# Two products of the first attention written in pairs with 64 columns of weights

## The chip, the cores and the metric

The kernel runs on one core of a Trainium2 chip. The metric is the device time of one execution in microseconds (us), as the median of several runs. A core has TensorE (in the profile PE for the matmuls and PEld for the loads of weights), VectorE (DVE), ScalarE (ACT), GpSimd (POOL) and SyncE (SP), each with a queue of instructions of its own, and 16 DMA engines. The engines meet through semaphores.

## The reference

Four attention blocks run one after the other over x of shape (64, 64, 128): 64 sequences of 64 tokens with 128 features. The change lies in the first of them, a cross attention with relative positions. Its core, cut to what matters:

```python
kv = jnp.concatenate([memory, layer_input], axis=1)          # 128 tokens: 64 of the memory, 64 of x
q = (layer_input @ Wq).reshape(b, q_len, n_head, d_head)     # 16 heads of 64
k = (kv @ Wk).reshape(b, kl, n_head, d_head)
v = (kv @ Wv).reshape(b, kl, n_head, d_head)
r = (pe @ Wr).reshape(kl, n_head, d_head)
ac = jnp.einsum('bqhd,bkhd->bhqk', q + content_bias, k)
bd = rel_shift(jnp.einsum('bqhd,khd->bhqk', q + position_bias, r))
attn = jax.nn.softmax((ac + bd) * (1.0 / np.sqrt(d_head)), axis=-1)
ctx = jnp.einsum('bhqk,bkhd->bqhd', attn, v).reshape(b, q_len, n_head * d_head)
out = layer_norm(layer_input + ctx @ Wo, ln1_g, ln1_b)
```

Its feed-forward part, a second block with two attentions, a third with a gate and a fourth with two attentions and a mixture of experts follow. They are not touched.

## The kernel before

The first attention walks over 32 tiles. A tile is two sequences, so 2 x 64 queries lie on the 128 partitions. The kernel doesn't compute v and the output projection one after the other. It multiplies Wv and Wo of each head once, at the start, into a table VO of 16 matrices of 128x128 (L598). For each tile it then needs, for head h and sequence b, the product of the tokens and the probabilities (128 features x 64 queries), and then the sum over the heads of that product times VO[h]. These two are the products that are changed:

- L536: for each half G of the heads (8 heads) and each sequence b, one f32 matmul with the tokens kv_in (128 tokens x 128 features) as weights and the probabilities of 8 heads x 64 queries, 512 columns, as the moving side. Four a tile; they write four banks of PSUM, j + 1 modulo 4. ScalarE copies each bank into pkvT (L749) and signals.
- L555: for each of the 16 heads one f32 matmul with pkvT[:, h] (128 features x 128 queries) as weights and VO[:, h] as the moving side, 128 columns. All sixteen add up in one bank. VectorE adds the sum to x (L690).

In the profile each f32 matmul has two records of a load and two of a matmul.

The order of TensorE's work is written out by hand in l0_tensor. A helper, walk_ahead, calls one function for each tile n; has(d) is true where tile n + d exists, so work for four tiles is in flight in one call. In a call TensorE does in this order: L499, 16 transposes of the probabilities of tile n; L515, the scores of tile n + 1, 32 products with 64 rows and 64 columns of weights, in all four quarters of the array; L528, two transposes of the tokens of tile n + 3; L536 for tile n; L548, 8 products with w_q for tile n + 3; L555 for tile n; L572, 16 products with 64 rows, for the relative positions of tile n + 3; L1199 (a helper for products in parts), the keys of tile n + 3, 24 records of 256 columns. The transposes at L528 and the products at L536 and L548 wait for semaphores of VectorE and ScalarE between them: probsT_kept (VectorE has copied the transposed probabilities, L663), kv_kept (VectorE has rounded the tokens into two parts, L675 and L679) and pkvT_kept. The first three calls and the last ones leave out what has no tile: tiles 0 to 28 have all parts, tiles 29 to 31 lack L528, L548, L572 and L1199, and tile 31 lacks L515 too. In the second attention L959 is a product that has 128 rows and 64 columns of weights already, after the transposes at L952.

The stage ends in a meeting of all engines (the function meet), and the next stage begins behind it.

Of the kernel before, what the change touches and what calls it, by code (L numbers as in the profile page):

```python
# [35 lines left out]
S = 64  # L36
D = 128
H = 16
# [110 lines left out]
def build(nc, a, out):  # L149
# [7 lines left out]
    with ctx:  # L157
        def sb(name, shape, dt=F32):
            return ctx.enter_context(nc.sbuf_tensor("sb_" + name, shape, dt))
# [3 lines left out]
        def sem(name):  # L163
            if name not in sems:
                sems[name] = ctx.enter_context(nc.semaphore("is_" + name))
            return sems[name]

        PS = ctx.enter_context(nc.psum_tensor("PS", [P, 8, 512], F32))
# [38 lines left out]
        with ExitStack() as first:  # L207
            VO, rel_bias, w_q0, w_k0_hi, w_k0_lo, rT, probs, probsT, pkvT = (
                first.enter_context(nc.sbuf_tensor("sb_" + name, shape, dt))
                for name, shape, dt in (("VO", [P, H, P], F32), ("rel_bias", [P, H, KL + 1], F32),  # L210
                                        ("w_q0", [P, H * DK], F32), ("w_k0_hi", [P, H * DK], F32R),
                                        ("w_k0_lo", [P, H * DK], F32R), ("rT", [P, H // 2, KL], F32),
                                        ("probs", [P, H, KL], F32), ("probsT", [P, H, P], F32),
                                        ("pkvT", [P, H, P], F32)))
# [119 lines left out]
        kv_in = sb("kv_in", [P, 4, 2, D])  # L334
# [120 lines left out]
        def l0_tensor(e, c):  # L455
# [9 lines left out]
            for q in range(2):  # L465
                o = bank()
                for i in range(4):
                    ch = 4 * q + i
                    ins = e.matmul(o[:, i * KL:(i + 1) * KL], wr[:, 2 * ch:2 * ch + 2], peT, start=True, stop=True)
                ins.then_inc(sem("l0_table_done"), 1)  # L470
            e.wait_ge(sem("l0_gap_wide"), 1)
            for g in range(4):
                o = bank()
                r = slice(DK * (g % 2), DK * (g % 2) + DK)
                if g == 0:
                    e.wait_ge(sem("l0_table_drained"), 2)
                for i in range(4):
                    ch = 4 * (g // 2) + i
                    ins = e.matmul(o[:, i * P:(i + 1) * P], gap_wide[r, ch], rT[r, ch], start=True, stop=True)
# [4 lines left out]
            def step(k, u, has):  # L484
# [3 lines left out]
                if has(0):  # L488
                    for g in range(4):
# [8 lines left out]
                        for i in range(4):  # L498
                            ins = e.transpose(PS[:, g, i * P:i * P + P], probs[:, 4 * g + i], ident[:, :])  # L499
                        ins.then_inc(sem("l0_probsT_done"), 1)  # L500
                if has(1):
# [3 lines left out]
                    for ch in range(H // 2):  # L505
                        i = ch % 4
                        for hh in range(2):
                            g, r = 2 * (ch // 4) + hh, slice(DK * hh, DK * hh + DK)
# [5 lines left out]
                            for b in range(2):  # L514
                                ins = e.matmul(PS[S * b:S * b + S, 4 + g, i * KL:i * KL + KL],  # L515
                                               q0T[r, v1, ch, S * b:S * b + S], k0T[r, v1, ch, KL * b:KL * b + KL],
                                               start=True, stop=True, skip_group_check=True)
                            if i == 3:
                                ins.then_inc(sem("l0_scores_done"), 1)
                if has(3):  # L520
# [6 lines left out]
                    for b in range(2):  # L527
                        ins = e.transpose(PS[:, 0, b * KL:b * KL + KL], kv_in[:, (u + 3) % 4, b], ident[:, :])  # L528
                    ins.then_inc(sem("l0_kvT_done"), 1)
                if has(0):  # L530
                    for j in range(4):
                        G, b = j // 2, j % 2
                        e.wait_ge(sem("l0_probsT_kept"), 2 * n + (1 if j == 0 else 2))
                        if j == 3 and has(3):
                            e.wait_ge(sem("l0_kv_kept"), 2 * (n + 3) + 2)
                        e.matmul(PS[:, (j + 1) % 4], kv_in[:, u, b], probsT[:, 8 * G:8 * G + 8, S * b:S * b + S],  # L536
                                 start=True, stop=True).then_inc(sem("l0_pkv_done"), 1)
                if has(3):
                    t = n + 3
                    e.wait_ge(sem("l0_kv_kept"), 2 * t + 1)  # L540
                    for half in range(2):
# [4 lines left out]
                        for i in range(4):  # L546
                            ch = 4 * half + i
                            ins = e.matmul(PS[:, 1 + half, i * P:i * P + P], w_q0[:, P * ch:P * ch + P], x_own,  # L548
                                           start=True, stop=True)
                        ins.then_inc(sem("l0_q_done"), 1)  # L550
                if has(0):
                    for j in range(H):
                        if j % 8 == 0:
                            e.wait_ge(sem("l0_pkvT_kept"), 4 * n + (3 if j == 0 else 4))
                        ins = e.matmul(PS[:, 3, 0:D], pkvT[:, j], VO[:, j], start=(j == 0), stop=(j == H - 1))  # L555
                    ins.then_inc(sem("l0_out_done"), 1)
                if has(3):
                    t = n + 3
                    for half in range(2):
                        e.wait_ge(sem("l0_q_kept"), 2 * t + half + 1)  # L560
                        for i in range(4):
                            ch = 4 * half + i
                            for hh in range(2):
                                g, r = 2 * half + hh, slice(DK * hh, DK * hh + DK)
                                if i == 0:
# [4 lines left out]
                                    elif has(2):  # L570
                                        e.wait_ge(sem("l0_rel_kept"), 4 * (n + 2) + g + 1)
                                ins = e.matmul(PS[:, 4 + g, i * KL:i * KL + KL], q0T[r, v3, ch], rT[r, ch],  # L572
                                               start=True, stop=True, skip_group_check=True)
# [3 lines left out]
                    for j in range(4):  # L577
# [8 lines left out]
                        for i in range(2):  # L586
                            at = P * (2 * j + i)
                            ins = product_in_parts(e, PS[:, j, 2 * KL * i:2 * KL * i + 2 * KL],
                                                   (w_k0_hi[:, at:at + P], w_k0_lo[:, at:at + P]),
                                                   (x_hi0[:, :], x_lo0[:, :]))  # L590
                        ins.then_inc(sem("l0_k_done"), 1)
                if isinstance(n, int) and n == -3:
                    e.wait_ge(sem("l0_vo_loaded"), 32)
                    for g in range(4):
                        e.wait_ge(sem("l0_rel_kept"), g + 1)
                        for i in range(4):
                            h = head_at(4 * g + i)
                            ins = e.matmul(PS[:, 4 + g, i * P:(i + 1) * P], wvT[:, h], wo0[:, h], start=True, stop=True)  # L598
                        ins.then_inc(sem("l0_table_done"), 1)
            walk_ahead(e, NT, step)  # L600
            e.wait_ge(sem("bases"), 1)
            for i, n in enumerate(("sa", "ca")):
                ins = e.matmul(PS[:, 2, P * i:P * i + P], bv_wide[:, i], w_out[n][:, :], start=True, stop=True)
# [592 lines left out]
        def product_in_parts(e, o, left, right):  # L1196

            for i, (l, r) in enumerate(((0, 0), (0, 1), (1, 0))):
                ins = e.matmul(o, left[l], right[r], start=(i == 0), stop=(i == 2))  # L1199
            return ins  # L1200
# [796 lines left out]
```

## Time and profile before

| | |
|---|---|
| median of 3 runs | 1948.61 us (1948.49 to 1951.13) |
| profiled execution | 1958.74 us |
| its span, first to last instruction | 1957.2 us |
| PE busy | 1623.2 us, 83% |
| PEld busy | 1297.1 us, 66% |
| DVE busy | 1360.1 us, 69% |
| ACT busy | 1171.2 us, 60% |
| POOL busy | 944.9 us, 48% |
| mean granted clock of TensorE | 0.904 |

The first attention takes about the first 620 us of the span. The profile gives the start of each instruction and its length; those of matmuls are pipelined, so the lengths of neighbours overlap, and the cost of one in a row is the distance of the starts. A row of the view in order of time merges neighbours of one kind: its first number is the start of the first, its second the time to the end of the last, and x is how many there are. Brackets at its end, if any, are idle time of the engine ahead of it.

### The profile page before, as it was taken

Reading aid. Unit: us, or ns where it says so; the run is one execution under the profiler, and the core shown is the slowest. Engines: PE = TensorE matmul, PEld = TensorE weight load, DVE = VectorE, ACT = ScalarE, POOL = GpSimd, SP = SyncE. Lnnn points to the kernel's source line nnn. Section 1 sums busy time; section 2 is a strip of 40 time slices with the busy share of each in tenths; the row PEclk is TensorE's granted clock in tenths of the full one; section 3 lists DMA queues with packets and bytes.
Section 4 is the critical chain, followed back from the end, with each engine's and each line's share of the span. In section 5 each row is a group of like instructions: output and inputs, shape, how many; then the busy total and the mean of one; then the engine's idle time right before and its main releaser. Section 6 shows DMA issues by size and latency. Waiting matters only on the chain. (4 is left out here: it accounts for less than half of the span.)

```text
span 1957.2 us, 54686 instructions
## 1 busy us (share of the span) xinstructions
PE 1623.2 (83%) x17114; PEld 1297.1 (66%) x17114; DVE 1360.1 (69%) x4172; ACT 1171.2 (60%) x3299; POOL 944.9 (48%) x1373
## 2 busy tenths in 40 slices
PE   6899999999996969999998764379998895439992
PEld 6788888888884747767776641157776674437771
DVE  3777777777775648888776538868887774337873
ACT  2776777677764437778776322258887771127771
POOL 2354344444532445556664424434454444646773
PEclk8999999999998979999998877779999995559996
DMA  8866666766661022230000000000000000136665
GB/s 228 159 149 144 155 148 139 160 142 153 146 148 45 0 103 106 100 110 21 19 18 8 1 1 1 0 4 1 0 10 13 12 9 21 43 99 206 220 211 163
DMA packets 214820, 167.19 MB, mean 85 GB/s; under 512 B 27633, under 2 KB 188785, under 8 KB 214449
## 3 DMA queue, kind: packets, MB, share of 16 engines
q1 hardware_dynamic: 206128, 142.88, 29.3%
q0 software_dynamic: 8576, 22.88, 3.6%
q8 instruction: 59, 0.97, 0.2%
q14 instruction: 57, 0.46, 0.1%
HBM read 91.92 MB, written 73.76 MB: 85 GB/s over the span
## 5 line engine op out<-in xcount | busy, mean ns | idle before, releaser
L738 ACT ACTIVATE sb_probs<-sb_probs,sb_work 128x128 f32<-128x128 f32 x512 | 198.6, 405 | 117.4 <-DVE sb_work L641 117.4
L281 POOL TENSOR_SCALAR sb_next_var_eps<-sb_next_moments 128x1 f32<-128x1 f32 (+1 forms) x184 | 45.3, 246 | 422.3 <-DVE sb_next_moments L721 241.9
L890 POOL TENSOR_TENSOR sb_work<-sb_work,sb_cols 128x512 f32<-128x512 f32 x128 | 134.1, 1048 | 216.2 <-ACT sb_work L1107 134.2
L1033 DVE TENSOR_REDUCE sb_work<-PS 128x8 f32<-128x512 f32 x256 | 175.2, 684 | 46.6 <-PE PS L932 44.9
L1035 DVE TENSOR_TENSOR sb_work<-PS,sb_work 128x512 f32<-128x512 f32 x256 | 177.0, 691 | 8.8
L1067 ACT ACTIVATE sb_work<-sb_work 128x512 f32<-128x512 f32 x256 | 161.5, 631 | 32.8 <-DVE sb_work L1035 26.8
L906 PE MATMUL PS<-sb_ident,sb_work 128*128 128x128 f32 x1024 | 151.0, 288 | 15.4 <-ACT sb_work L1107 9.9
L959 PEld LDWEIGHTS PS<-sb_v_ones,sb_work 128*64 128x64 f32 x4096 | 133.0, 140 | 24.0 <-issue 15.8
L959 PE MATMUL PS<-sb_v_ones,sb_work 128*64 128x18 f32 x4096 | 144.9, 214 | 4.3 <-ACT sb_work L1073 2.8
L1073 ACT ACTIVATE sb_work<-PS 128x512 f32<-128x512 f32 x256 | 139.6, 595 | 10.3 <-PE PS L906 7.0
L906 PEld LDWEIGHTS PS<-sb_ident,sb_work 128*128 128x128 f32 x1024 | 115.0, 146 | 42.7 <-issue 30.5
L433 POOL TENSOR_TENSOR sb_work<-sb_rel_bias,sb_work 128x2064 f32<-128x2064 f32 x32 | 134.7, 4210 | 5.2 <-POOL sb_work L431 4.2
L285 POOL TENSOR_TENSOR sb_tile_inv_std<-sb_next_var_eps,sb_half_power 128x1 f32 (+3 forms) x184 | 118.6, 644 | 7.2 <-POOL sb_next_var_eps L281 0.2
L555 PE MATMUL PS<-sb_VO,sb_pkvT 128*128 128x128 f32 x1024 | 119.9, 275 | 0.0
L1849 POOL DMA_INDIRECT expert_outs<-sb_work x92 | 96.5, 1049 | 47.3 <-issue 37.6
L555 PEld LDWEIGHTS PS<-sb_VO,sb_pkvT 128*128 128x128 f32 x1024 | 116.9, 192 | 2.3 <-ACT sb_pkvT L749 2.3
L536 PE MATMUL PS<-sb_probsT,sb_kv_in 128*128 128x512 f32 x256 | 117.3, 602 | 0.4 <-DVE sb_probsT L663 0.4
L641 DVE CUSTOM_DVE_ANT_0 sb_probs<-PS,sb_work 128x128 f32<-128x128 f32 x512 | 112.4, 285 | 4.2 <-DMA sb_work<-rel_scratch 4.2
L738 ACT ACTIVATION_READ_ACCUMULATOR sb_probs<-sb_probs,sb_work 128x1 f32 x512 | 104.4, 204 | 0.0
L771 ACT ACTIVATE sb_work<-PS 128x512 f32<-128x512 f32 x128 | 76.2, 598 | 44.7 <-PE PS L1199 34.0
L656 DVE TENSOR_TENSOR sb_work<-PS,sb_work 128x512 f32<-128x512 f32 x128 | 79.6, 683 | 32.8 <-PE PS L572 26.5
L1825 DVE CAST sb_h_hi<-sb_work 128x512 fp32r<-128x512 f32 x92 | 57.8, 628 | 53.9 <-ACT sb_work L1801 50.5
(276 smaller groups left out, 4454.4 us busy)
## 6 DMA issues: line engine op xcount, KB each, us to landing
rel_scratch<-sb_work SPq DMA_DIRECT2D x64, 516.0 KB, 7.8
sb_work<-rel_scratch SPq DMA_DIRECT2D x64, 512.0 KB, 6.6
expert_rows<-sb_blank SPq DMA_DIRECT2D x36, 520.0 KB, 2.9
sb_w_up<-expert_halves SPq DMA_DIRECT2D x23, 512.0 KB
sb_w_down<-expert_halves SPq DMA_DIRECT2D x23, 512.0 KB
expert_halves<-sb_e_halves POOLq DMA_DIRECT2D x16, 512.0 KB, 6.1
sb_work<-expert_rows SPq DMA_DIRECT2D x23, 260.0 KB
sb_e_raw<-e_W POOLq DMA_DIRECT2D x16, 256.0 KB, 5.5
```

The source lines that it names most:

```text
L285: e.tensor_tensor(inv_std[:, bass.ds(t0, tiles)], var_eps[:, 0:tiles], half_power[:, 0:tiles], ALU.pow)\
L433: e.tensor_tensor(masked_bias, rel_bias[:, :, :], mask_f.unsqueeze(1).to_broadcast([P, H, KL + 1]), ALU.add)\
L536: e.matmul(PS[:, (j + 1) % 4], kv_in[:, u, b], probsT[:, 8 * G:8 * G + 8, S * b:S * b + S], start=True, stop=True).then_inc(sem("l0_pkv_do ...
L555: ins = e.matmul(PS[:, 3, 0:D], pkvT[:, j], VO[:, j], start=(j == 0), stop=(j == H - 1))
L738: ins = e.activation(probs[:, j], probs[:, j], ACT.Exp, bias=neg_max[:, j:j + 1], scale=-1.0, accum_out=row_sum[:, j:j + 1])
L890: e.tensor_tensor(k_masked[:, u3], k_sb[:, u3].rearrange("p (b k) -> p b k", b=2).unsqueeze(2) .to_broadcast([P, 2, 4, S]), col("place").u ...
L906: ins = e.transpose(PS[:, 4 + j, i * P:i * P + P], att_probs[:, u, 8 * j + 2 * i:8 * j + 2 * i + 2], ident[:, :])
L959: ins = e.matmul(values[S * b:S * b + S, 2 * i:2 * i + 2], att_probsT[:, i, S * b:S * b + S], v_ones[:, u, b, 2 * i:2 * i + 2], start=True ...
L1033: e.tensor_reduce(top, mine, AX.X, ALU.max).then_inc(sem("att_max_ready"), 1)
L1035: e.tensor_tensor(by_group(att_probs[:, v])[:, 2 * j:2 * j + 2], mine, top.unsqueeze(3).to_broadcast([P, 2, 4, S]), ALU.subtract)\
L1067: e.activation(att_probs[:, v, 8 * j:8 * j + 8], att_probs[:, v, 8 * j:8 * j + 8], ACT.Exp, scale=front["scale"]).then_inc(sem("att_exp_do ...
L1073: e.activation(att_probsT[:, 4 * j:4 * j + 4].rearrange("p i q -> p (i q)"), PS[:, 4 + j], ACT.Copy)\
```

## The change

At L536 each product is cut in two along the features: the first takes the tokens' features 0 to 63 as weights and writes partitions 0 to 63 of the bank, the second takes features 64 to 127 and writes partitions 64 to 127. The moving side is the same 512 columns for both. The signal is given by the second. At L555 each product is cut in two along the queries, which are one sequence each: 64 columns of pkvT as weights, 64 partitions of the sum as output, with the same VO[:, j] as moving side. What is computed is the same, and no wait is added or taken away.

```diff
-                        e.matmul(PS[:, (j + 1) % 4], kv_in[:, u, b], probsT[:, 8 * G:8 * G + 8, S * b:S * b + S],
-                                 start=True, stop=True).then_inc(sem("l0_pkv_done"), 1)
+                        for half in range(2):
+                            r = slice(D // 2 * half, D // 2 * half + D // 2)
+                            ins = e.matmul(PS[r, (j + 1) % 4], kv_in[:, u, b, r], probsT[:, 8 * G:8 * G + 8, S * b:S * b + S],
+                                           start=True, stop=True, skip_group_check=True)
+                        ins.then_inc(sem("l0_pkv_done"), 1)
...
-                        ins = e.matmul(PS[:, 3, 0:D], pkvT[:, j], VO[:, j], start=(j == 0), stop=(j == H - 1))
+                        for b in range(2):
+                            ins = e.matmul(PS[S * b:S * b + S, 3, 0:D], pkvT[:, j, S * b:S * b + S], VO[:, j],
+                                           start=(j == 0), stop=(j == H - 1), skip_group_check=True)
```

## Rows read from the trace of the kernel before

**Rows 1.** The page: the span in 40 slices, busy tenths and granted clock of PE.
```profile
PE   6899999999996969999998764379998895439992
...
PEclk8999999999998979999998877779999995559996
```

**Rows 2.** Busy time of each engine in one stretch, with granted clock and DMA.
```profile
core 0: us, PE busy (x) PEld busy (x) DVE busy (x) ACT busy (x) POOL busy (x), PEclk, DMA share, GB/s
100.00:500.00 400.00, 400.00 (x4357) 342.22 (x4356) 301.56 (x1204) 283.88 (x1071) 188.42 (x210) 1.00 0.67 149
```

**Rows 3.** Waits of PEld, 200 to 500 us: total, times, longest (PE has none).
```profile
PEld PS L536 <- issue: 18.5, 80, 0.2
...
PEld PS L536 <- DVE sb_x_lo L679: 6.5, 17, 0.6
```

**Rows 4.** PE in order of time, L555 of one tile to L555 of the next.
```profile
304.14 3.74 PE L555 MATMUL PS<-sb_VO,sb_pkvT 128*128 128x128 f32 x32
307.81 2.06 PE L572 MATMUL PS<-sb_rT,sb_work 64*128 64x128 f32 x32
309.80 0.39 PE L1199 MATMUL PS<-sb_x_hi,sb_w_k_hi 128*128 128x256 f32 x1
...
312.75 1.91 PE L499 MATMUL PS<-sb_ident,sb_probs 128*128 128x128 f32 x16
314.59 1.98 PE L515 MATMUL PS<-sb_work 64*64 64x128 f32 x64
316.50 0.44 PE L528 MATMUL PS<-sb_ident,sb_kv_in 128*128 128x128 f32 x2
316.77 3.60 PE L536 MATMUL PS<-sb_probsT,sb_kv_in 128*128 128x512 f32 x8
320.20 1.95 PE L548 MATMUL PS<-sb_work,sb_w_q 128*128 128x128 f32 x16
321.99 1.28 PE L555 MATMUL PS<-sb_VO,sb_pkvT 128*128 128x128 f32 x10
```

**Rows 5.** By line, 200 to 500 us: duration ns min/median/max.
```profile
L515 PE MATMUL PS<-sb_work x1088: 269/269/321, 207.4 to 494.8; 64*64 64x128 f32 x182
...
L572 PE MATMUL PS<-sb_rT,sb_work x544: 272/272/373, 200.6 to 488.1; 64*128 64x128 f32 x182
...
L536 PE MATMUL PS<-sb_probsT,sb_kv_in x136: 592/592/659, 209.6 to 498.3; 128*128 128x512 f32 x136
...
L555 PE MATMUL PS<-sb_VO,sb_pkvT x518: 275/275/275, 199.8 to 486.1; 128*128 128x128 f32 x173
...
L528 PE MATMUL PS<-sb_ident,sb_kv_in x34: 272/300/329, 209.3 to 495.2; 128*128 128x128 f32 x34
...
L1199 PE MATMUL PS<-sb_x_hi,sb_w_k_hi x136: 279/282/390, 202.6 to 490.9; 128*128 128x256 f32 x136
```

**Rows 6.** Records in 0.05 us: L515, L959; columns as in rows 2, PE and PEld.
```profile
314.57:314.62 0.05, 0.03 (x4) 0.04 (x4) 1.00 0.77 175
...
1001.13:1001.18 0.05, 0.04 (x2) 0.04 (x2) 1.00 0.00 0
```

**Rows 7.** PE in order of time, L952 and L959; then L959 by line there.
```profile
1000.94 0.27 PE L952 MATMUL PS<-sb_ident,sb_work 128*128 128x128 f32 x1
1001.14 1.11 PE L959 MATMUL PS<-sb_v_ones,sb_work 128*64 128x18 f32 x32
...
L959 PE MATMUL PS<-sb_v_ones,sb_work x32: 211/211/232, 1001.1 to 1002.0; 128*64 128x18 f32 x32
```

**Rows 8.** L536 in order of time in the last two tiles, 30 and 31.
```profile
597.82 3.70 PE L536 MATMUL PS<-sb_probsT,sb_kv_in 128*128 128x512 f32 x8
...
609.92 5.40 PE L536 MATMUL PS<-sb_probsT,sb_kv_in 128*128 128x512 f32 x8 [0.44 <-DVE sb_probsT L663]
```

**Rows 9.** The loads (PEld) of L536's fourth product, in order of time.
```profile
318.97 0.19 PEld L536 LDWEIGHTS PS<-sb_probsT,sb_kv_in 128*128 128x128 f32 x1 [0.29 <-DVE sb_x_lo L679]
319.35 0.19 PEld L536 LDWEIGHTS PS<-sb_probsT,sb_kv_in 128*128 128x128 f32 x1 [0.19 <-issue]
```

## The prediction

> **What bounds the kernel now.** I read the slices of the page first. The first attention lies in the first third of the span, and there TensorE (PE) is at nine tenths or more in nearly every slice, at full clock (the 9s of PEclk) [rows 1]. Then one stretch of 400 us in the middle of this stage: PE 400.00 of 400.00 us, granted clock 1.00, VectorE 301.56, ScalarE 283.88, GpSimd 188.42, DMA 0.67 [rows 2]. A busy PE is not yet a bound PE, because the ends of matmuls are modelled, so I looked for waits. In 200 to 500 us the view has none of PE itself. PEld (the loads) stands idle 18.5 us for "issue" on L536 and 6.5 us for VectorE's L679, in 17 pieces [rows 3]. These are loads that stand ready behind a long stream (L536 streams 0.43 us, its load takes 0.19), so they cost PE nothing. The third proof is the pace itself. In order of time one tile goes L499, L515, L528, L536, L548, L555, L572, L1199, and L555 starts at 304.14 and again at 321.99, that is 17.85 us per tile, and no row has an idle piece in brackets [rows 4]. So each 0.1 us that PE gains or loses in a tile of this loop moves the end of the stage by 0.1 us, as often as the loop is full. The stage ends in a meeting of all engines, so nothing later takes it back.
>
> **What a record costs.** An f32 product is two PE records. Pace = (busy of the group minus the length of one record) / (records minus 1). L555: (3.74 - 0.275)/31 = 0.112 us per record. L548: (1.95 - 0.275)/15 = 0.112. L499: (1.91 - 0.273)/15 = 0.109. L536, 512 columns: (3.60 - 0.592)/7 = 0.430 [rows 4, 5]. 0.430/512 is 0.84 ns per column, so 128 columns need 0.107 us for the stream alone, whatever the weights are. L515 works in tiles of 64x64, L572 in tiles of 64x128 and L959 (second stage) in 128x64, the form that the change uses. Members of a group start together: in 0.05 us there are four records of L515 and two of L959 [rows 6]. L515's 64 records are 16 groups of four: (1.98 - 0.27 - 0.02 - 0.05)/15 = 0.109 us per group, where 0.02 is the stagger in a group and 0.05 is explained below. L572's 16 pairs: (2.06 - 0.27 - 0.01 - 0.10)/15 = 0.112 [rows 4, 5]. So tiles do run side by side, but a group costs what one full-array record costs.
>
> **What a change of tile shape costs.** This is the heart of it. Where no shape changes, the next group starts in step: L536 to L548 (320.20 - 316.77)/8 = 0.429, L548 to L555 (321.99 - 320.20)/16 = 0.112 [rows 4]. Where it changes there are two losses. First, the gap: L499 to L515 takes 314.59 - 312.75 = 1.84 for 16 records that need 16 x 0.109 = 1.75, so 0.09 more; L555 to L572 takes 3.67 for 32 x 0.112 = 3.58, again 0.09; L952 to L959 takes 0.20 where 0.11 is the pace, again 0.09 [rows 4, 7]. Second, the load of the first record is not hidden. The first record is longer than the others by what its load has to do: L515 321 against 269 (0.05, 64 columns of weights), L572 373 against 272 (0.10, 128 columns), L1199 390 against 282 (0.11, 128 columns), L528 329 against 272 (0.06, a transpose) [rows 5], L959 232 against 211 (0.02, 64 columns) [rows 7]. The end of the loop has it for L536 itself: behind L515 its eight records take 3.70 instead of 3.60 [rows 4, 8].
>
> The Trainium skill states this in "TensorEngine Tiling (Array Packing)", Tiling Modes: changing the mode, not only the tile, drains the engine. By that rule the change cannot be free here, and the trace agrees, with its 0.09 us; if shapes changed for nothing, the sum would be the small gain of (5) below alone, -0.08 us per tile and 1946 us. [...]
>
> **The change part by part.**
> (1) L536, probabilities times tokens: four products (eight records of 512 columns) become eight (sixteen records in eight pairs). A pair streams the same 512 columns, so 0.43 us per pair, as before, plus one stagger of 0.01. The loads get shorter, 64 columns, but they were hidden behind 0.43 us of stream. Gain 0.
> (2) Entering it from L528, which stays a full-array transpose: new change of shape, 0.09 + 0.05 (64 columns, as L515). Between 0.11 (with L959's 0.02) and 0.20 (with L572's 0.10). I take 0.14: the stream behind the load is long, as in L515.
> (3) Leaving it for L548, full array and 128 columns of weights: new, 0.09 + 0.10 = 0.19. Between 0.15 (L528's 0.06) and 0.20 (L1199). I take 0.19, L536 behind L515 being the same kind of load.
> (4) Entering L555 from L548: new, 0.14, bounds as in (2), plus a stagger of 0.01.
> (5) L555, 16 products (32 records of 128 columns) become 32 in 16 pairs (32 pair records). Its pace was 0.112; the stream's floor is 0.107, and L515, which has 64-column loads and 128-column streams, goes at 0.109. Gain 32 x 0.003 = 0.08. Bounds: 0 (pace as L572) and 0.16 (pace 0.107). I take L515's, the same sizes.
> (6) L555 to L572: a change of shape already, now from another shape. 0.
> (7) PE's other instructions: 8 + 32 more matmuls with their loads in a tile. L515 issues four loads and four matmuls per 0.109 us [rows 4], the pairs need half of that. 0. Waits and signals stay; each signal hangs on the last product of its pair, which ends 0.01 us later.
> Sum per tile: 0.14 + 0.01 + 0.19 + 0.14 + 0.01 - 0.08 = 0.41 us, so 17.85 becomes 18.26. The low end is 0.11 + 0.15 + 0.11 - 0.16 = 0.21. The high end is 0.20 + 0.20 + 0.20 = 0.60, with no gain in (5).
>
> Full tiles are those that have L548 behind L536, tiles 0 to 28 of 32: 29 x 0.41 = 11.9 us. Tiles 29 and 30 have L515 directly ahead of L536 and L555 directly behind [rows 8], so the shape changes there anyway, with a shorter load (0.05 less), then none, then L555 0.08 less, then a new change to L499 (0.09 + 0.06): about 0. The last tile adds one entry and one exit, of which part lies in waits that PE has there (0.44 us ahead of L536 [rows 8]): 0.3. Sum 12.2 us.
>
> **What is late next.** Nothing. VectorE, ScalarE and GpSimd are idle for 25, 29 and 53% of the stage [rows 2]. The one signal that is near is VectorE's L679, which releases the fourth product of L536: its load comes at 318.97, at 0.29 us after the engine was free, needs 0.11, and the stream behind it begins at 319.35 [rows 9], 0.27 us later than it could. In some tiles this is just too late: the longest record of L536 took 659 ns against 592 [rows 5]. The change delays that stream by 0.15 us and leaves L679's own start where it was, so this can only get better (0.2 us in all, not counted). The granted clock is at its level of 2.4 GHz in this stage and PE gets more to do, not less [rows 2].
>
> **Against the medians.** The profiled execution had a span of 1957.2 us and 1958.74 in all, the runs without the profiler a median of 1948.61, which is 0.5% less. The sum is one of instruction times in a stage at constant clock, so I add it to both: 1958.74 gives 1970.9, 1948.61 gives 1960.8.
>
> **Rivals.**
> (A) Faster. If L555's 0.112 were set by the load of 128 columns and not by the stream, loads of 64 columns in parallel would bring the pace of a pair toward L959's, which is (1.11 - 0.21 - 0.03)/15 = 0.058 [rows 7]. That is 32 x 0.054 = 1.73 us gained per tile against 0.49 of changes of shape, -1.2 us x 29 = -36 us: 1913 us. It wins from a pace under 0.112 - 0.49/32 = 0.097. Against it: L515 has the short loads and still needs 0.109, and L536 shows 0.107 for 128 columns. L959 streams only 18 columns. 5%.
> (B) Streams of two 128x64 tiles don't run side by side when they are long (all 128 rows are read twice, from the same addresses). L959's pairs start together but their 18 columns prove little. Then a pair of L536 takes 0.86 and one of L555 0.22: 8 x 0.43 + 32 x 0.107 = 6.9 us x 32 = 220 us, 2180 us. Against it: L515's groups of four include two column tiles on each half of the rows, each with its own stream, at full pace. 3%.
> (C) The loads of a pair are not hidden, since both members lie on the same rows: 0.05 us on each of 40 pair records, 2 us a tile, 64 us on top of the forecast's 12, 2025 us. Against it: L555 and L499 hide their loads on the same rows today, and L959's pace of 0.058 is less than a load of 0.05 and a stream of 18 x 0.84 ns = 0.015 together. 3%. The Trainium skill says in "TensorE: Matmul & The Clock Gate", Part 3, that loads overlap running matmuls only where the row group differs, which would give this case; the trace speaks against it, with L555's 0.112.
> (D) No difference. The loss of 0.09 may belong to changes of rows and not of columns, or the program may keep the full array's shape, or the cost hides in time that PE has. Against it: L952 to L959 changes columns alone and shows the gap, and PE shows no wait. Under 0.13 us per tile (3.9/29) it would be within what can be told, so about 1949. 5%.
>
> **How the numbers follow.** Forecast 84%: 1960.8. Its terms' ends, 0.21 and 0.60 per tile, times 29 and with 0 to 0.3 at the end give 6.1 to 17.7 us, 1954.7 to 1966.3. The three runs differ by 2.6 us among themselves, but not all terms will stand at one end, so I take 1955 to 1967. That holds nearly all of the forecast's own 84% and nothing of the rivals, about 8 in 10. A measurement of this kernel can tell 0.2%, 3.9 us, from no change. Slower 84 + 3 + 3 = 90%, same 5%, faster 5%.
>
> **What the changed profile would show.** L536 and L555 as 128*64 forms with twice the records, two starting together; L536's eight pairs still 0.43 apart and L555's at 0.109; the first record of L536 and L555 0.05 longer, L548's first 0.10 longer; gaps of 0.09 more at three places; 18.26 us from L555 to L555; all later stages shifted and otherwise equal. The forecast is wrong if L555's pace is far from 0.109 (A or C), if L536's pairs are not 0.43 apart (B), or if the first records are no longer than the rest (D).

## The result and the profile after

The changed kernel takes 1983.33 us (median of 4 runs, 1980.89 to 1985.28) where the kernel before takes 1949.87 on the same chip: a ratio of 1.0161, interval 1.0137 to 1.0185. It is slower, as forecast, but by 33.5 us and not by 11 to 12, and 1983.33 lies far outside 1955 to 1967.

First what went as forecast. PE in order of time for one full tile after the change (start us, length us, line; L538 is what L536 was, L551 what L548 was, L559 what L555 was, L577 and L1204 what L572 and L1199 were), to be held against [rows 4]:

```profile
300.98 3.71 PE L559 MATMUL PS<-sb_VO,sb_pkvT 128*64 128x128 f32 x64
304.62 2.06 PE L577 MATMUL PS<-sb_rT,sb_work 64*128 64x128 f32 x32
...
309.56 1.91 PE L499 MATMUL PS<-sb_ident,sb_probs 128*128 128x128 f32 x16
...
313.31 0.44 PE L528 MATMUL PS<-sb_ident,sb_kv_in 128*128 128x128 f32 x2
313.68 3.66 PE L538 MATMUL PS<-sb_probsT,sb_kv_in 128*64 128x512 f32 x16
317.26 2.05 PE L551 MATMUL PS<-sb_work,sb_w_q 128*128 128x128 f32 x16
319.25 2.29 PE L559 MATMUL PS<-sb_VO,sb_pkvT 128*64 128x128 f32 x38
```

From L559 to L559 it is 319.25 - 300.98 = 18.27 us, against a forecast of 18.26. By piece, the distance of starts after minus before: L528 to L538 0.37 - 0.27 = +0.10, L538 to L551 3.58 - 3.43 = +0.15, L551 to L559 1.99 - 1.79 = +0.20, L559 to L577 3.64 - 3.67 = -0.03. Sum +0.42. A load that isn't hidden lengthens the first record of its group, so it shows in the distance to the next group. Sorted that way the forecast's terms are 0.09, then 0.05 + 0.01 + 0.09 = 0.15, then 0.10 + 0.09 = 0.19, then 0.05 + 0.01 - 0.08 = -0.02: each is right to 0.01. The same by line, duration in ns min/median/max, from 300 to 358 us, to be held against [rows 5]:

```profile
L538 PE MATMUL PS<-sb_probsT,sb_kv_in x48: 592/592/644, 313.7 to 353.3; 128*64 128x512 f32 x48
...
L551 PE MATMUL PS<-sb_work,sb_w_q x58: 275/275/378, 299.8 to 355.6; 128*128 128x128 f32 x58
...
L559 PE MATMUL PS<-sb_VO,sb_pkvT x232: 272/273/323, 301.0 to 357.9; 128*64 128x128 f32 x116
```

The first record of L538 is 0.05 longer than the rest, that of L551 0.10, that of L559 0.05. L538's pairs are still (3.66 - 0.59 - 0.06)/7 = 0.430 apart, L559's (3.71 - 0.27 - 0.06)/31 = 0.109.

Now what did not. The slices of PE on the page after show nothing of it: those of the loop are all 9s, as before. But its table of DMA queues has a row that differs, and so have the waits of PE from 100 to 600 us. The kernel before has only one there, of 2.0 us for VectorE, behind the loop in tile 30. The row and the waits are now (us in total, times, longest):

```profile
q8 instruction: 112, 1.84, 0.4%
```
```profile
PE PS L499 <- issue: 12.6, 5, 2.7
PE PS L515 <- issue: 1.0, 1, 1.0
```

On the page of the kernel before that row was:

```profile
q8 instruction: 59, 0.97, 0.2%
```

q8 carries code in packets of 16 KB (0.97 MB/59), and they keep step with TensorE's instructions: in the two kernels that are written out below (experiments 1 and 10) one comes every 260 and every 254 traced instructions of TensorE. I count 256 to a packet. Before, the last one comes at 195.9 us, in the first pass of the loop, and the next at 569.0, behind it; after, they come all the time. The queues in 280 to 360 us (packets, MB, share), first before, where there is no q8, then the row that the kernel after has besides these two:

```profile
q1 hardware_dynamic: 20323, 10.00, 58.9%
q0 software_dynamic: 528, 1.84, 7.8%
```
```profile
q8 instruction: 10, 0.16, 1.0%
```

The five waits are one for each jump back. TensorE's loop is one jump for four tiles (walk_ahead writes tiles 0 to 3 and 28 to 31 out and loops over 4 to 27), so it jumps back five times, ahead of tiles 8, 12, 16, 20 and 24. The first (tile 8), PE in order of time, and the row of two stretches there with the granted clock (columns as in [rows 2], the clock behind POOL):

```profile
212.72 3.29 PE L499 MATMUL PS<-sb_ident,sb_probs 128*128 128x128 f32 x16 [2.67 <-issue]
```
```profile
212.10:215.40 3.30, 2.68 (x13) 2.69 (x14) 0.68 (x1) 0.00 (x0) 2.49 (x4) 0.50 0.76 172
215.50:217.50 2.00, 2.00 (x61) 1.83 (x63) 1.90 (x5) 0.00 (x0) 2.00 (x1) 1.00 0.78 202
```

PE stands for 2.67 us ahead of L499. "issue" says that no engine and no transfer of the kernel was waited for. Then L499's 16 records take 3.29 us where they take 1.91 in the tile above, another 1.38. This second part is the clock: the granted clock is 0.50 there, the level of 1.2 GHz, and 1.00 again behind it. The stall ahead of tile 16 has the same wait and no such fall:

```profile
367.02 1.96 PE L499 MATMUL PS<-sb_ident,sb_probs 128*128 128x128 f32 x16 [2.51 <-issue]
...
370.53 1.54 PE L515 MATMUL PS<-sb_work 64*64 64x128 f32 x48 [0.95 <-issue]
```
```profile
367.00:369.60 2.60, 2.56 (x32) 2.25 (x33) 1.46 (x2) 0.00 (x0) 2.18 (x3) 1.00 0.76 172
```

Here L499 runs at its usual pace, and PE waits a second time, 0.95 us, in the middle of L515. From L559 to L559 the tiles with the jump take 22.46, 22.42, 22.16, 22.70 and 22.70 us, 4.2, 4.2, 3.9, 4.4 and 4.4 over 18.26, in sum 21.1 us. With 29 x 0.41 = 11.9 that is the 33 us. Of the 21.1 us, 13.6 are idle time of PE (the waits above). The clock fell at four of the five jumps (not at tile 16), and these four tiles lost 1.5 to 1.9 us besides their idle time, tile 16 lost 0.4: about 5 to 6 us of the 21 are the clock, by my estimate. The length of the stage, from the first start of L499 in tile 0 to the last in tile 31, says the same: 546.5 us before, 580.0 after, 33.5 more, of which 32.9 lie in the 29 full tiles.

### The profile page after: what moved, and what is told of

The parts are those of the page before. It is cut to its first block and busy times, and to the rows that moved or that the text cites. A ratio compares the mean times of both kernels' runs of the same rounds, so it can differ in the third digit from the quotient of the medians.

```text
span 1982.6 us, 57246 instructions
## 1 busy us (share of the span) xinstructions
PE 1634.7 (82%) x18394; PEld 1279.7 (65%) x18394; DVE 1357.3 (68%) x4172; ACT 1175.5 (59%) x3299; POOL 937.2 (47%) x1373
## 5 line engine op out<-in xcount | busy, mean ns | idle before, releaser
L559 PE MATMUL PS<-sb_VO,sb_pkvT 128*64 128x128 f32 x2048 | 118.9, 274 | 0.1
L538 PE MATMUL PS<-sb_probsT,sb_kv_in 128*64 128x512 f32 x512 | 117.6, 601 | 0.0
L559 PEld LDWEIGHTS PS<-sb_VO,sb_pkvT 128*64 128x64 f32 x2048 | 111.1, 137 | 6.1 <-ACT sb_pkvT L754 2.6
```

What stands on the lines that cost most here:

```text
L538: ins = e.matmul(PS[r, (j + 1) % 4], kv_in[:, u, b, r], probsT[:, 8 * G:8 * G + 8, S * b:S * b + S], start=True, stop=True, skip_group_che ...
L559: ins = e.matmul(PS[S * b:S * b + S, 3, 0:D], pkvT[:, j, S * b:S * b + S], VO[:, j], start=(j == 0), stop=(j == H - 1), skip_group_check=True)
```

## The experiments

Ratios are with their 95% intervals, always against the kernel before on the same chip; three groups of runs were on chips where it took 1961.35, 1961.36 and 1951.76 us. "Stage" is the length defined above, in the profiled execution. In copies of the kernel that have more lines at the start, L499 is L500 or L505.

The theories. F: TensorE's code for the loop no longer stays near the engine, and is fetched again at each jump back. P is its sharper form: what counts is how many packets of 256 instructions the loop touches. S is the other form: what counts is the loop's length. R, the rival: the stall comes from the pairs or from the data of these tiles.

**1. The changed kernel with TensorE's loop written out.**

```diff
-            walk_ahead(e, NT, step)
+            walk_in_line(e, NT, step)
```

walk_in_line calls step for every n from -3 to 31 and has no loop on the chip.

> The changed kernel, with TensorE's loop over the tiles of the first attention written out in full; the other engines keep their loops. Theory F (the loop's code no longer stays near the engine and is fetched again at each jump back): no jump, so no stall of 4 us at every fourth tile, 18.26 us from tile to tile throughout, 5 x 4.2 = 21 us less than the changed kernel, 1962 us, and the fetches of code run on steadily. Rival R (the stall belongs to the data, to a semaphore of another engine or to the pairs themselves at tiles 8, 12, 16, 20, 24): the stalls stay, 1983 us.

Ratio 1.0076 (1.0052 to 1.0101), 1973.78 against 1961.35 us, so 12.4 us over the kernel before where the changed kernel had 33.5. All 29 full tiles take 18.26 or 18.27 us, together 11.7 us more than before (forecast 11.9). The stage is 559.8 us, 13.3 more: the other 1.5 us lie in tile 30, where the granted clock was 0.50 from 605.5 to 608.7 us. The trace of experiment 2, which turned out to be the program before, has the same there (0.50 from 594.7 to 597.9 us), so this part isn't the change. The place of the first jump, tile 8, is now:

```profile
207.27 1.91 PE L505 MATMUL PS<-sb_ident,sb_probs 128*128 128x128 f32 x16
```

and code is fetched steadily, 9 packets in 280 to 360 us, with no wait of PE from 100 to 600 us. So fetching as such costs nothing as long as it runs straight ahead. R falls, F stands, and the prediction's cost of the full tiles is what is left when the jumps are gone.

**2. The kernel before with 80 empty instructions a tile.**

```diff
                                  start=True, stop=True).then_inc(sem("l0_pkv_done"), 1)
+                        for _ in range(20):
+                            e.nop(nofuse=True)
```

> The kernel before, with 20 empty instructions behind each of the four products of L536 on TensorE, 80 a tile and 320 in the loop of four tiles, so the loop is as long as that of the changed kernel (1957 instructions) and no tile shape changes. Theory F: 17.85 us within the four tiles, if the empty instructions hide behind the streams of 0.86 us, and about 4.2 us more at each jump back, 1949.9 + 21 = 1971 us, with code fetched all through the stage. Rival R: no stall, 1950 us, or evenly more where the empty instructions cost time themselves.

Ratio 0.9987 (0.9971 to 1.0003), no stall. But the run says nothing: the trace has 1637 instructions of TensorE in four tiles as before, and q8 has 59 packets as before, 15 of them ahead of the first jump back, though 4 of the tiles there are written out and would have been longer. The empty instructions were not in the program.

**3 and 4. One part of the change alone.** L536 in pairs (the first half of the diff), and L555 in pairs (the second half).

> Only the first part of the change (L536 in pairs). My step sizes give 0.09 + 0.05 + 0.01 on entering and 0.19 on leaving, 0.35 us a tile: 18.20 us from tile to tile, 29 x 0.35 = 10 us, 1960 us. The loop has 1637 + 64 = 1701 instructions. Theory F says no more than that the stall of 4 us comes or not by the size: with it 1981 us, and its place tells a bound for the size. A rival that lays the stall on the long pairs of 512 columns wants it here and not in the run with the second part alone.

Ratio 1.0162 (1.0134 to 1.0191), 1992.96 against 1961.35 us. Tile to tile 18.19 us (forecast 18.20), with five stalls, in sum 21.1 us.

> Only the second part of the change (L555 in pairs). By my step sizes 0.09 + 0.05 + 0.01 on entering, 0.08 gained by the pace, nothing new on leaving: 0.07 us a tile, 17.92 us from tile to tile, 1952 us. The loop has 1637 + 256 = 1893 instructions, nearer to the changed kernel's 1957, so by theory F the stall of 4 us is likelier here than with the first part alone: with it 1973 us.

Ratio 1.0094 (1.0066 to 1.0122), 1979.64 against 1961.35 us. Tile to tile 17.91 us (forecast 17.92), again five stalls, in sum 24.5 us (3.4 to 6.9 each) in the profiled execution, which was the longest of its four. The median is 18.3 us over the kernel before.

Both parts stall, with 1701 and with 1893 instructions in the loop. That they do so with quite different products, and one of them with hardly a longer loop than before (1637), is against R. The cost of a tile is right to 0.01 us for each part alone.

**5 to 7. The loop moved.** To part P from S, code is added ahead of the loop and the loop is not touched. What is added are repeats of the eight products of L469 in the setup, into the same place; four instructions each.

```diff
-                for i in range(4):
+                for i in range(24):
+                    i = i % 4
```

This is the move by 160 instructions; range(28) gives 192.

> The kernel before, with 160 more instructions of TensorE ahead of the loop: the eight products of L469 at the very start are made six times over instead of once, into the same place. The loop itself is untouched, 1637 instructions. The code comes in packets of 16 KB, 256 instructions. From the fetches I count that the loop now begins just behind the start of a packet and lies in 7 of them, and that 160 instructions further on it would lie in 8. Theory P (what counts is how many packets the loop touches, 7 stay and 8 don't): stalls of about 4 us at tiles 8, 12, 16, 20 and 24, 20 us more, 1970 us against 1950, or 1982 on a chip where before takes 1961, and code fetched all through the stage. Theory S (what counts is the length of the loop, with the border between 1637 and 1701 instructions): no stall, 17.85 us throughout, only what the added products cost at the start, 0 to 20 us in the setup. Rival R (the stall comes from the pairs): no stall.

Ratio 0.9987 (0.9970 to 1.0003): no stall, 17.85 us from tile to tile (17.87 to 17.93 in the five that the kernel before has a little longer too), no fetch behind the first pass of the loop.

> Only the first part of the change (L536 in pairs, 1701 instructions in the loop, 4 us of stall at each jump back), with 192 more instructions ahead of the loop (the eight products of L469 seven times over). Theory P: the loop begins just behind the start of a packet again and lies in 7 packets, so the stalls go away: 18.19 us throughout, 20 us less than without the move, and no fetches in the loop. Theory S and rival R: the stalls stay.

Ratio 1.0146 (1.0122 to 1.0170): the stalls stay, in sum 21.0 us.

> Only the second part of the change (L555 in pairs, 1893 instructions in the loop), with the same 192 instructions ahead of the loop. 1893 instructions are 7.4 packets and lie in 8 at least, so theory P expects the stalls here wherever the loop begins, as theory S does. If they went away here as well, it would be the move and not the number of packets.

Ratio 1.0117 (1.0083 to 1.0151), of two executions only: the stalls stay, in sum 17.4 us in the profiled one.

The first two results are what S expected and not what P did. But P had said two things: that packets count, and where they lie. The second was a guess, that the code starts with the first instruction of the trace. The fetches test it. Each is made where TensorE enters a new packet: 15 come before the kernel before jumps back the first time, behind 3960 traced instructions, and 16 in the kernel moved by 160, behind 4120. If c instructions stand ahead of the traced ones, all four cases fit P for c between 76 and 135. Instructions numbered from the start of the program, at 256 a packet:

| kernel | loop's instructions | from | to | packets | stalls |
|---|---|---|---|---|---|
| before | 1637 | 2324 + c | 3960 + c | 9 to 15, 7 | no |
| before, moved by 160 | 1637 | 2484 + c | 4120 + c | 10 to 16, 7 | no |
| tokens in pairs | 1701 | 2388 + c | 4088 + c | 9 to 16, 8 | yes |
| tokens in pairs, moved by 192 | 1701 | 2580 + c | 4280 + c | 10 to 17, 8 | yes |

The count gives the changed kernel packets 10 to 18, nine of them, and the table in pairs 10 to 17 and, moved by 192, 11 to 18, eight each; all three stall. Neither the place where a loop begins in its packet nor that of the jump decides alone: by the same numbers the tokens in pairs moved by 192 begin as far behind the start of a packet as the kernel before (96 to 155 instructions), and the table in pairs jumps as far behind one as it does (196 to 255), and both stall. But c was fitted after the runs, so the count had to forecast something new.

**8 and 9. Two moves that the count tells apart.**

```diff
-                for i in range(4):
+                for i in range(4 * (3, 3)[q]):
+                    i = i % 4
```

This is the move by 64 instructions; (5, 4) in place of (3, 3) gives 112.

> The kernel before with 64 more instructions of TensorE ahead of the loop (the eight products of L469 made three times over). The move by 160 gave no stall and the first part of the change moved by 192 kept it. Counting packets of 256 instructions, both fit theory P if the code has 76 to 135 instructions ahead of those that the trace shows: before lies in packets 9 to 15 (15 fetches up to the first jump back), before moved by 160 in 10 to 16 (16 fetches), the first part of the change in 9 to 16 (a new packet is entered just ahead of the jump and packet 9 is gone), moved by 192 in 10 to 17. By the same count the loop of before, moved by 64, lies in 9 to 16, 8 packets. Theory P: stalls of about 4 us at tiles 8, 12, 16, 20 and 24 in the kernel before, whose loop is untouched, about 20 us more, code fetched all through. Theory S (the length of the loop alone, border between 1637 and 1701 instructions): no stall, no difference.

Ratio 1.0138 (1.0111 to 1.0164), 1979.00 against 1951.76 us: 27 us slower, with the loop of the kernel before, to the letter. The stage has 23.5 us of them, 23.8 in the five tiles with a jump; the other 4 us of the medians stay unexplained. The first jump back, PE in order of time (the granted clock is 0.50 from 207.9 to 211.2 us), and the waits from 100 to 600 us:

```profile
208.31 3.37 PE L500 MATMUL PS<-sb_ident,sb_probs 128*128 128x128 f32 x16 [3.24 <-issue]
```
```profile
PE PS L500 <- issue: 15.1, 5, 3.2
PE PS L516 <- issue: 2.5, 3, 1.3
```

Its q8 on the page, with as many packets as the kernel with the tokens in pairs has:

```profile
q8 instruction: 104, 1.70, 0.4%
```

> Only the first part of the change (L536 in pairs, 1701 instructions in the loop), moved by 112 instructions (the first four products of L469 five times, the other four four times). By the count of packets it then lies in 10 to 16, 7 packets. Theory P: no stall, 18.19 us throughout, 20 us less than the same edit without the move: 10 us over the kernel before. Theory S: the stalls stay, 31 us over the kernel before.

Ratio 1.0066 (1.0043 to 1.0088), 1964.56 against 1951.76 us: 12.8 us slower. The stage is 557.6 us, 11.1 more than before, where the same edit without the move had 32.2 more; in both, 1.5 of this lie in tile 30 at a granted clock of 0.50 for part of it, as in experiment 1. The 29 full tiles took 9.6 us more here and 30.7 without the move. The place of the first jump back, and q8:

```profile
207.21 1.91 PE L500 MATMUL PS<-sb_ident,sb_probs 128*128 128x128 f32 x16
```
```profile
q8 instruction: 60, 0.98, 0.2%
```

18.18 to 18.20 us from tile to tile, with no exception. A loop of 1637 instructions stalls and a longer one of 1701 doesn't, by nothing but its place. S falls. That the stall comes in a kernel without pairs is against R once more. P forecast both runs and fits all the others: three kernels with 7 packets hold their loop, five with 8 and one with 9 don't. Runs 5 and 6 had the right mechanism and the wrong place.

**10. The kernel before written out.** The edit is that of experiment 1.

> The kernel before, with TensorE's loop written out in full. All theories: 17.85 us throughout, no stall; the 0.03 to 0.07 us that each jump back costs today goes, 0.2 us in all, so no change that can be told. If writing out had a price or a gain of its own, the run of the changed kernel in line would have to be read with it.

Ratio 0.9986 (0.9974 to 0.9998), the stage 546.7 us against 546.5. It fetches 31 packets in 200 to 560 us and waits for none. The writing out has no price and no gain that the stage shows. The expectation had one thing wrong: the 0.03 to 0.07 us were not the price of a jump back. In the kernel before, L499 starts 0.12 us behind the last record of L1199, across a jump as elsewhere; what these five tiles have over 17.85 (0.02 to 0.07 us) lies ahead of L536's last product, and the kernel written out has it too (0.08 to 0.14 us) without any jump of TensorE. The medians are 2.8 us lower than before. If the change were priced by the medians of the two kernels written out (1973.78 and 1958.52, on two chips), it would be 15.3 us and not 12.4; so it is the full tiles, 11.7 us, that bear out the forecast of 11.9, and what the other 3 us are is open.

## Why the prediction was wrong

- **The bound** was right. PE had no air, and what the tiles got longer is in the total: 33.5 us of the stage, 33.5 us of the medians. That these agree to a tenth is luck: the two profiled executions differ by 25.4 us in span, 33.5 more in the stage and 8 less outside it.
- **The cost of a record and of a change of tile shape** (0.09 us of gap, 0.05 or 0.10 of load that isn't hidden) was right, part by part and in sum: 18.27 for 18.26, with one part alone 18.19 for 18.20 and 17.91 for 17.92. So were (1) to (6): the full tiles cost 11.7 us in experiment 1 against 11.9. The 0.3 us of the last tiles can't be told, for traces of one program differ by 1.5 us there with the granted clock.
- **Step (7) failed.** It asked what 40 more matmul records with 40 more loads a tile cost in issue, found that L515 issues twice as fast, and wrote 0. It did not ask where these instructions lie. They are 80 a tile, 320 in the loop, 1.25 packets of code. The loop went from 6.4 to 7.6 packets, and a loop of 7.6 touches 8 at least wherever it lies (here 9, by the count above), more than the 7 that stay. So it was not bad luck of the place; with the tokens in pairs alone (6.6 packets) it would have been. Measured: five stalls of 3.9 to 4.4 us, 21 us, almost twice the whole sum.
- **The clock** was part of that miss. The prediction had it at 2.4 GHz throughout, because PE would get more to do. The stalls took that away: behind four of the five waits the granted clock was 0.50 for a while, and L499 took 3.29 us for 1.91. It is about a quarter of the 21 us (the estimate above).
- **The profile of before had it in view.** The table of DMA queues on its page has the 59 packets of q8, and the same view of 280 to 360 us has no q8 at all: the loop ran without fetching code. I read the DMA only as a share of 0.67. With these and a count of 1637 instructions, "the loop grows by a packet and a quarter and may be fetched at each jump" would have been a rival with five stalls to price. Its size could not have been read from this trace, for it shows no such jump in the stage.
- **Rivals A to D** did not come. L559's pace is 0.109, so A and C are out, L538's 0.430 is against B, and the three changes of shape cost what they cost elsewhere, against D. The range held what was uncertain in the terms and nothing of a term that wasn't there; the 90% for slower stood on reasons that held.
- Small things: L536's fourth product, released by L679, did get more air, as said: the five tiles that were 0.02 to 0.07 us longer ahead of it are gone in experiment 1. No other engine took PE's place.

## What to carry to other kernels

When an edit adds instructions to a loop, count them against the packets of code that the loop touches (256 instructions each here), and look in the queues' table whether code is fetched while the loop runs. If it isn't, the loop is held, and a packet more, or the same loop somewhat further on, may cost microseconds at every jump back; a loop of few passes is then better written out (experiment 1: 1973.78 us, where the loop took about 21 us more). Look at the granted clock behind such a wait, too: its fall can add to the price. And a pair of half-width products in place of one full-width gains nothing while the stream of columns sets the pace, but pays for each change of tile shape, in and out.

## What the runs showed of the hardware

- TensorE held a loop of 1637 to 1701 instructions when it lay in 7 packets of 256, and the jump back then cost nothing that a trace shows (L499 0.12 us behind L1199, as elsewhere). It fetched the loop anew in each pass when it touched 8 or 9 (30 jumps in six kernels: 3.4 to 5.4 us at 26 of them, 1.8 to 6.9 over all). 64 instructions ahead of an untouched loop decide it: 1979.00 against 1951.76 us.
- A stall at a jump has up to three parts, seen in the changed kernel. PE stands ahead of L499 (2.67 us at tile 8). At some jumps it stands again ahead of or in L515 (0.95 us at tile 16). And at 20 of the 30 jumps the granted clock fell to 0.50 around the restart: L499 took 3.29 us for 1.91 at tile 8 and 1.96 at tile 16, where the clock stayed at 1.00. In the kernels that held their loop it stayed at 1.00 in all full tiles.
- Part of the fetch is hidden. In the changed kernel's trace the first branch is read at 207.9 us, while PE still works on L1204 until 210.05; packets start at 208.2 and 208.9, and L499 starts at 212.72. So 4.8 us pass from the branch to the first product, and PE is idle for 2.67 of them.
- Straight code is fetched without a price here: 31 and 37 packets in 200 to 560 us in the two kernels written out, before and after, and PE waits for none.
- The Trainium skill, "Runtime: NRT & Kernel Launch", Instruction fetch mechanics, gives TensorE a memory of 128 KiB for code, 2048 instructions, refilled in blocks of 16 KiB, and says that a taken branch to a target outside the window stalls for a fetch. The runs agree with the blocks (0.97 MB in 59 packets) and with the stall. That 7 of the 8 blocks stay would fit one of them being read ahead, and so would the fetches of one pass, on average 9 for the tokens in pairs with 8 packets and 10 for the changed kernel with 9; that is argued, not shown. The same section also speaks of a window of two blocks only; for TensorE the runs show 7.
- Tiles of 128x64 run in pairs at full pace with streams of 128 and of 512 columns (0.109 and 0.430 us a pair), which L959 with its 18 columns had left open.
- Not tried: whether the stall shrinks when the 16 DMA engines are less busy (0.67 in this stage), why the clock fell at some jumps and not at others, and which instructions the c ahead of the trace are.
